# Selective scan with a ternary feed-forward block on one core: softplus, FFN high parts and silus given to other engines

## The reference

```python
xr = x @ in_w.T;  xx, res = split(xr, 2)              # 512 + 512 channels
xx = silu(conv4(xx) + conv_b)                          # causal, 4 taps, per channel
delta, B, C = split(xx @ xproj_w.T, [16, 32])
delta = softplus(delta @ dt_w.T + dt_b)                # 512 channels
state = exp(delta * A) * state + delta * B * xx        # 16 states per channel, 512 steps
y = sum_over_states(state * C) + xx * D
x = layernorm(x + (y * silu(res)) @ out_w.T)
h = silu(lin(x, w1)) * lin(x, w2)                      # ternary weights, 1024 hidden
h = gelu(lin(h, h1)); h = gelu(lin(h, h2))
x = layernorm(x + lin(h, w3))
```

## Time and profile before

| | |
|---|---|
| time, median of 3 runs | 3149.71 us |
| profiled execution: its time, its span | 3155.72 us, 3153.9 us |
| PE busy | 2583.1 us (82%) |
| DVE busy | 2621.1 us (83%) |
| ACT busy | 2343.3 us (74%) |
| POOL busy | 1071.0 us (34%) |
| mean granted clock of TensorE | 0.897 |
| ACT table loads in the profile | 194 |

### The profile page before, as it was taken

How to read it: one execution, slowest core, us unless ns; L and a number is a source line. 1 busy time by engine, 2 the same in 40 slices (tenths; PEclk the granted TensorE clock), 3 DMA queues, 4 the chain that set the end, 5 groups by cost and what they waited for, 6 DMA issues and landing times.

```text
span 3153.9 us, 41504 instructions
## 1 busy us (share of the span) xinstructions
PE 2583.1 (82%) x12290; PEld 1944.8 (62%) x12290; DVE 2621.1 (83%) x2625; ACT 2343.3 (74%) x3653; POOL 1071.0 (34%) x1028
## 2 busy tenths in 40 slices
PE   4355788888888888988888898888888889898888
PEld 1223566676666666676666766666676756666666
DVE  3678998989898897989889898988989898998830
ACT  2776687877969787796968779697877969687822
POOL 0112333333433433343343334234333423423432
PEclk8566899999989999999989999899999989899999
DMA  1996787787878778787887878787787878778933
GB/s 52 290 321 140 167 193 180 185 197 184 194 179 193 190 181 186 183 194 183 190 188 179 194 181 194 179 196 189 178 190 181 200 186 196 189 180 191 229 111 110
DMA packets 230192, 585.49 MB, mean 186 GB/s; under 512 B 26016, under 2 KB 26400, under 8 KB 229808
## 3 DMA queue, kind: packets, MB, share of 16 engines
q0 software_dynamic: 73728, 268.47, 46.2%
q1 hardware_dynamic: 119344, 246.86, 22.4%
q10 hardware_dynamic: 36864, 67.13, 7.9%
HBM read 281.93 MB, written 31.98 MB: 100 GB/s over the span
## 4 chain that ended last, share of the span: by engine, by line
PE 32%; DVE 29%; ACT 17%; issue 14%; DMA 4%; ACTq 1%; DVEq 1%; SPq 1%; POOL 1%; POOLq 0%
PE ffn_ps L479 17%; DVE scan_ps L782 11%; DVE hC L792 5%; PE scan_ps L367 5%; ACT dB L616 4%; ACT dA L607 3%; DVE y L806 3%; PE misc_ps L372 3%; DMA x<-ffn_w 3%; PE misc_ps L423 2%; DVE gate L899 2%; PE misc_ps L460 2%; PE misc_ps L408 2%; ACT L607 2%; PE misc_ps L367 2%
## 5 line engine op out<-in xcount | busy, mean ns | idle before, releaser
L782 DVE TENSOR_TENSOR_SCAN scan_ps<-dA,scan_ps 128x1024 f32<-128x1024 f32 x512 | 1170.8, 2287 | 57.0 <-PE scan_ps L367 33.2
L968 POOL DMA_DIRECT2D y<-hC x512 | 446.1, 871 | 1811.2 <-DVE hC L792 1735.1
L367 PE MATMUL scan_ps<-ident,dB 128*128 128x128 f32 x4096 | 613.4, 300 | 375.7 <-DVE hC L792 292.3
L367 PEld LDWEIGHTS scan_ps<-ident,dB 128*128 128x128 f32 x4096 | 519.9, 154 | 521.2 <-DVE hC L792 305.5
L616 ACT ACTIVATE dB<-duT,bT 128x512 f32<-128x512 f32 x1024 | 726.4, 711 | 154.5 <-PE scan_ps L367 153.2
L607 ACT ACTIVATE dA<-delta,a_neg 128x512 f32<-128x512 f32 (+1 forms) x1024 | 710.1, 712 | 41.1 <-DVE hC L792 38.0
L479 PE MATMUL ffn_ps<-hb_hi,ring 128*128 128x512 f32 x1536 | 660.1, 430 | 18.4 <-DVE gate L899 8.7
L792 DVE TENSOR_TENSOR hC<-scan_ps,c_rows_sb 128x1024 f32<-128x1024 f32 x512 | 623.6, 1218 | 49.8 <-DMA y<-hC 41.5
L479 PE MATMUL ffn_ps<-hb_lo,ring 128*128 128x512 f32 x1536 | 620.7, 404 | 0.0
L479 PE MATMUL ffn_ps<-ha_hi,ring 128*128 128x512 f32 x1024 | 443.5, 433 | 2.4 <-POOL ha_lo L990 2.4
L479 PE MATMUL ffn_ps<-ha_lo,ring 128*128 128x512 f32 x1024 | 407.7, 398 | 0.0
(11 more groups left out here) (90 smaller groups left out, 2941.9 us busy)
## 6 DMA issues: line engine op xcount, KB each, us to landing
y<-hC POOLq DMA_DIRECT2D x512, 512.0 KB, 5.8
ring<-split_weights SPq DMA_DIRECT2D x704, 256.0 KB, 4.3
c_rows_sb<-c_rows ACTq DMA_DIRECT2D x256, 256.0 KB, 4.0
xt<-x_tok SPq DMA_DIRECT2D x32, 512.0 KB, 6.1
x<-ffn_w SPq DMA_DIRECT2D x22, 512.0 KB, 9.7
split_weights<-ha_hi SPq DMA_DIRECT2D x22, 512.0 KB, 5.2
split_weights<-ha_lo SPq DMA_DIRECT2D x22, 512.0 KB, 7.0
out_tok<-out_st SPq DMA_DIRECT2D x16, 512.0 KB, 2.9
```

The costliest lines, as they stand in the source:

```text
L367: mm = nc.tensor.transpose(dst[:, j * P:(j + 1) * P], src(j), ident[:])
L782: nc.vector.tensor_tensor_scan(b, dA[:, a:a + 2, :].rearrange("p a l -> p (a l)"), b, 0.0, ALU.mult, ALU.add).then_inc(scan_done, 1)
L968: pool.dma_start(y2[:, par, c:c + 2, :], hC[:, p % 2], accum_op=ALU.add).then_inc(y_added[p % 2], 16)
```

## The change

Three regroupings, and the tables moved to suit them.

1. Both silus of the mixer use ScalarE's `Silu` and need no DVE product. The convolution's silu is done for four tiles at one step, `F_U` = 38. The halvings of weights that went with tanh are gone.
2. The softplus loses its DVE work except 1+e and its rounding loss. ACT reads dt from PSUM twice, as |x+b| and as relu(x+b). POOL subtracts the loss, adds the ln, multiplies by u, and multiplies u by D.
3. The FFN's high parts are copied by POOL, just before it subtracts them.

```diff
-T_RES, T_GATE = (0, 3, 6, 8), (2, 5, 7, 10)
+T_RES, T_GATE = (2, 4, 7, 9), (4, 5, 9, 10)
-A_HI, A_LO = 2, 3
+A_LO = 2
-LO_AFTER = 1
+LO_AFTER = 0
+F_U = 38
-F_DELTA, F_DELTA_U, F_Y, F_DU = (54, 54, 55, 55), (54, 54, 55, 55), (57, 58, 59, 60), (56, 57, 58, 59)
+F_DELTA, F_DELTA_U, F_Y, F_DU = (52, 52, 53, 53), (53, 53, 54, 54), (57, 58, 59, 60), (56, 57, 58, 59)
-NO_EXP = {s % TILES for s in GELU_AT}
+NO_EXP = {s % TILES for s in GELU_AT} | {F_U} | set(T_GATE)
...
+                if s == F_U:
+                    for c in range(DC):
+                        act.wait_ge(conv_taps, r * (DC * (TAPS - 1)) + (c + 1) * (TAPS - 1))
+                        nc.scalar.activation(y2[:, par, c, :], y2[:, par, c, :], ACT.Silu).then_inc(u_ready, 1)
...
+                if s - 1 in F_DT:
+                    c = F_DT.index(s - 1)
+                    act.wait_ge(pe_dt, r * DC + (c + 1))
+                    nc.scalar.activation(du[:, c, :], misc_ps[:], ACT.Abs, bias=ch[:, c, C_DTB:C_DTB + 1]
+                    nc.scalar.activation(delta2[:, par, c, :], misc_ps[:], ACT.Relu, bias=ch[:, c, C_DTB:C_DTB + 1]
+                                         ).then_inc(dt_ready, 1)
...
-                    nc.scalar.activation(gate[:, c % 2, :], misc_ps[:], ACT.Tanh).then_inc(v_tanh, 1)
+                    nc.scalar.activation(gate[:, c % 2, :], misc_ps[:], ACT.Silu).then_inc(v_ready, 1)
...
+            def front_step(r, par, s):                      # on POOL
+                    if F_SUB[c] == s:
+                        nc.gpsimd.tensor_tensor(delta2[:, par, c, :], delta2[:, par, c, :], du[:, c, :], ALU.subtract
+                    if F_DELTA[c] == s:
+                        nc.gpsimd.tensor_tensor(delta2[:, par, c, :], delta2[:, par, c, :], sp_w[c], ALU.add
+                    if F_DELTA_U[c] == s:
+                        nc.gpsimd.tensor_tensor(du[:, c, :], y2[:, par, c, :], delta2[:, par, c, :], ALU.mult
+                    if F_Y[c] == s:
+                        nc.gpsimd.tensor_tensor(y2[:, par, c, :], y2[:, par, c, :],
+                                                ch[:, c, C_D:C_D + 1].to_broadcast([P, SEQ]), ALU.mult
...
+            def split_tile(f, i):                           # on POOL
+                nc.gpsimd.tensor_copy(hi[:, i % HC, :], x32[:, i % X32, :]).then_inc(ffn_hi, 1)
                 pool.wait_ge(ffn_hi, f * FFN_TILES + (i + 1))
                 nc.gpsimd.tensor_tensor(lo[:, i % HC, :], x32[:, i % X32, :], hi[:, i % HC, :].bitcast(F32),
                                         ALU.subtract).then_inc(ffn_lo, 1)
```

More of the change, by code:

```diff
@@ L629, in front_step @@
                     act.wait_ge(pe_xx, r * DC + (c + 1))
[L630 to L635 removed]
+                    nc.scalar.activation(y2[:, par, c, :], misc_ps[:], ACT.Identity, bias=ch[:, c, C_CONVB:C_CONVB + 1],
+                                         scale=ch[:, c, TAPS - 1:TAPS]).then_inc(conv_base, 1)
+                if s == F_U:
+                    for c in range(DC):
+                        act.wait_ge(conv_taps, r * (DC * (TAPS - 1)) + (c + 1) * (TAPS - 1))
+                        nc.scalar.activation(y2[:, par, c, :], y2[:, par, c, :], ACT.Silu).then_inc(u_ready, 1)
                 if s == F_DBL_OUT:
@@ L643, in front_step @@
                                          ACT.Copy).then_inc(bT_ready, 1)
-                for c in range(DC):
-                    if F_EXP[c] != s:
-                        continue
-                    act.wait_ge(dt_ready, r * DC + (c + 1))
-                    nc.scalar.activation(du[:, c, :], delta2[:, par, c, :], ACT.Abs).then_inc(sp_abs, 1)
+                if s - 1 in F_DT:
+                    c = F_DT.index(s - 1)
+                    act.wait_ge(pe_dt, r * DC + (c + 1))
+                    nc.scalar.activation(du[:, c, :], misc_ps[:], ACT.Abs, bias=ch[:, c, C_DTB:C_DTB + 1]
+                                         ).then_inc(sp_abs, 1)
+                    nc.scalar.activation(delta2[:, par, c, :], misc_ps[:], ACT.Relu, bias=ch[:, c, C_DTB:C_DTB + 1]
+                                         ).then_inc(dt_ready, 1)
                     act.wait_ge(sp_abs, r * DC + (c + 1))
@@ L689, in gelu_tiles @@
                                          scale=fs[:, 2 + i // HC, i % HC:i % HC + 1]).then_inc(gelu_x32, 1)
-            def hi_tiles(f, tiles):
-                for i in tiles:
-                    act.wait_ge(gelu_x32, f * (2 * HC) + (i + 1))
-                    if i == HC:
-                        act.wait_ge(pe_half, f * HALVES + 2 * HC)
-                    dst = hb_hi if i < HC else ha_hi
-                    nc.scalar.activation(dst[:, i % HC, :], x32[:, i % X32, :], ACT.Copy).then_inc(ffn_hi, 1)
             def ffn_step(f, s):
@@ L876, in tail_step @@
             def tail_step(r, par, s):
-                if s in T_GATE:
-                    c = T_GATE.index(s)
-                    dve.wait_ge(v_tanh, r * DC + (c + 1))
-                    nc.vector.scalar_tensor_tensor(out=gate[:, c % 2, :], in0=gate[:, c % 2, :], scalar=1.0,
-                                                   in1=misc_ps[:], op0=ALU.add, op1=ALU.mult).then_inc(v_ready, 1)
                 if s in T_ADD:
@@ L968, in y_pair @@
                 pool.dma_start(y2[:, par, c:c + 2, :], hC[:, p % 2], accum_op=ALU.add).then_inc(y_added[p % 2], 16)
+            def front_step(r, par, s):
+                for c in range(DC):
+                    if F_SUB[c] == s:
+                        pool.wait_ge(dt_ready, r * DC + (c + 1))
+                        pool.wait_ge(sp_lost, r * DC + (c + 1))
+                        nc.gpsimd.tensor_tensor(delta2[:, par, c, :], delta2[:, par, c, :], du[:, c, :], ALU.subtract
+                                                ).then_inc(sp_base, 1)
+                for c in range(DC):
+                    if F_DELTA[c] == s:
+                        pool.wait_ge(sp_base, r * DC + (c + 1))
+                        pool.wait_ge(sp_ln, r * DC + (c + 1))
+                        nc.gpsimd.tensor_tensor(delta2[:, par, c, :], delta2[:, par, c, :], sp_w[c], ALU.add
+                                                ).then_inc(delta_ready, 1)
+                for c in range(DC):
+                    if F_DELTA_U[c] == s:
+                        pool.wait_ge(u_ready, r * DC + (c + 1))
+                        pool.wait_ge(delta_ready, r * DC + (c + 1))
+                        nc.gpsimd.tensor_tensor(du[:, c, :], y2[:, par, c, :], delta2[:, par, c, :], ALU.mult
+                                                ).then_inc(du_ready, 1)
+                for c in range(DC):
+                    if F_Y[c] == s:
+                        pool.wait_ge(pe_dbl, r + 1)
+                        pool.wait_ge(du_ready, r * DC + (c + 1))
+                        nc.gpsimd.tensor_tensor(y2[:, par, c, :], y2[:, par, c, :],
+                                                ch[:, c, C_D:C_D + 1].to_broadcast([P, SEQ]), ALU.mult
+                                                ).then_inc(y_init, 1)
             def gate_tile(r, par, c):
@@ L1013, in iteration @@
                         ffn_step(end, s + TILES)
+                    if front is not None:
+                        front_step(front, fpar, s)
             iteration(-1, 1)
```

82 lines of the change are left out of this document (21 added, 61 removed).

## The result

The changed kernel takes 3212.14 us (median of 4 runs, 3209.38 to 3215.86) against 3150.68 of the kernel before in the same comparison: a ratio of 1.020, with a 95% interval of 1.0182 to 1.0218. It is 61 us slower. The forecast was 26 us slower. The profiled span grew by less, 53.6 us, from 3153.9 to 3207.5: the profiled execution of the kernel before was the slowest of its four.

What follows compares the result with a forecast made beforehand. No engine is full; a cycle of stretches in which engines take turns sets the row. -1.0 + 0.8 + 1.2 = +1.0 us a row, +15 over 15 rows, ends +12: +27, 3176 us on the median's scale, range 3103 to 3232.

Steps and rivals of the forecast that it cites:

- POOL's start: Softplus end: POOL takes the split of tile 6 at about 1351.2, with the gelus ending near 1351.7.
- PE's clock: PE's stretch behind `du`: longer idling makes it begin at half rate, +0.8 us a row, from 0 to 1.9.
- DVE's stretch and the PE stretch: Steps 15 to 31 and 32 to 50: work leaving DVE shortens neither, 0 us a row.
- ACT's earlier gelus: Before the softplus end: copies leave ACT, so the gelus end near 1351.7 instead of 1354.04.
- Softplus end: From the last gelus to `du`: `du` ready 1.0 us a row earlier, from -1.9 to +0.4.
- POOL's chain: Softplus end: two copies, two subtractions, eight operations and one transfer's issue on POOL take 14.8 us.
- Gates: Gate stretch: PE's last projection waits for the third silu, +1.2 us a row, from -1.2 to +3.
- Ends: Start and tail of the program, where nothing hides the chain or the loads: +6.4 and +6 us, together +12.
- Signs: Tests: DVE busy 330 us less, POOL operations 1.25 each, `du` transposes near gelu 7 plus 14.5, 278 loads, PE's silu wait.
- A: Four gate tiles: DVE's part ends the gate stretch, so its relief makes the kernel faster, 3116 us; chance 0.27.
- B: POOL's copy is as dear as its subtraction and the cycle waits for POOL, +3.6 a row, 3216 us; chance 0.15.
- C: ACT's table loads cost a drain beside their row, four in the full stretch adding 5.2 a row, 3255 us; chance 0.03.

Runs made afterwards that it cites:

- Experiment 9: Changed kernel with the subtraction of the rounding loss (four a row) back on DVE: 3197.0 us, 1.0142 of the kernel before.
- experiment 8: Kernel before with the softplus part of the change alone, high parts staying on ACT and gates by tanh: 3195.92 us, 1.0141 of the kernel before.
- Experiment 5: Changed kernel with filler products of constants on PE before its wait for `du`: 3187.65 us with eight, 3178.33 us with four.
- experiments 2 and 4: First: changed kernel with gates back to tanh at the old steps, 3155.98 us. Second: kernel before with only the high parts copied by POOL, 3097.88 us.
- experiment 6: Changed kernel with the gate silus at the steps of the kernel before, and exps allowed at those steps: 3169.78 us, 1.0059 of the kernel before.

## Why the prediction was off

Two steps failed: POOL's start at the softplus end, which was put before gelu 7 ends, and the term for PE's clock, which was too small. By the steps of the prediction, per row and against the table:

- **DVE's stretch and the PE stretch.** DVE's relief was put at nothing in steps 15 to 31, and it is 0.2. ACT's earlier gelus were put at -2.3; measured -2.9. Right, though ACT's list as the prediction counts it is only 1.6 shorter, so the 2.3 stands there without a source.
- **Softplus end.** Forecast: `du` 1.0 earlier than before, so the ln-to-`du` stretch about 1.3 longer. Measured: 3.0 longer. POOL's chain itself was right, 14.8 forecast and 14.8 measured. Its start was wrong. I let it begin 0.5 before gelu 7 ends, and it begins 1.1 behind: POOL had first to get through a split, a subtraction and a transfer's issue, queued behind a wait of 2.3 for DVE's product with C. (Just ahead of that product DVE's rounding loss took 1.66 instead of 0.69 beside a subtraction on POOL, from 1360.17; no run took this away alone.) I had listed what moved to POOL, but not what stood in its list just ahead. Experiment 9 points to the wait, and not to one operation more or less in the queue; the wait itself was not varied. Even with the start as forecast the stretch from the ln to `du` would have been 1.3 longer than before, and experiment 8 shows that POOL's chain costs time also where it starts with the ln. (One bound was miscounted: with the copy at 0.19 the sum gives -1.8, not -1.9.)
- **PE's clock.** This is the term that was mis-sized most. Forecast +0.8, from 0 to 1.9; measured +2.3, above its range. The term was priced from one projection of four matmuls, but the lower level lasted for the whole first part of the stretch, and the wait before it grew to 4.72. Experiment 5 settles it: 34 us of the 61. The trace of before could have told. First the changed kernel behind the softplus end, then the kernel before at the joint that the term was taken from:

```profile
1381.20:1388.00 6.80, 4.84 (x15) 3.96 (x16) 3.63 (x3) 1.81 (x3) 5.70 (x6) 0.50 0.60 120
```

```profile
1294.00:1300.80 6.80, 5.68 (x11) 3.10 (x10) 5.96 (x7) 3.58 (x6) 3.85 (x4) 0.50 0.53 116
```

Both stretches are at half rate throughout (clock 0.50), with PE busy 4.84 us and 5.68 us. Half of that, 2.4 and 2.8 us, is an estimate of what the level costs, where the prediction stopped at the 1.9 of the first four matmuls. The measured cost was 2.4.

- **Gates.** Forecast +1.2, measured +1.7. The mechanism, PE waiting for the third silu, was right: "PE has a wait of 3 to 4 us for the silu before its last projection" is the row with 3.14. That the size is near has some luck in it. By experiments 2 and 4 it is the difference of two larger terms: the silus cost 3.4 and the copies gave back 1.6. From the end of the third silu to the output projection the forecast had 6.9, and in the row shown it is 9.1 (1431.14 to 1440.25), of which 1.6 are the slower projection and transposes; this clock was in the upper bound, not in the sum.
- **Ends.** The start was forecast at +6.4. At the first transposes of `du` the changed kernel is 7.4 behind, but at the first sum behind the output projection only 1.4 (330.8 against 329.4), so most of this is made up within the first row. At the last transposes of `du` it is 51.0 behind, at the end 53.6: the tail, forecast at +6, is +2.6.
- **Signs.** Of those named, 278 loads, eight operations of some 1.25 and the wait for the silu came. The transposes of `du` came 16.0 behind gelu 7, not within 1 us of 14.5, and DVE's busy time fell too little.
- **Rivals.** A (faster) named PE's wait for the silu as its test, and it failed it. B was near in time (3216), but for the wrong reason: the copy is cheap, and layer 1 did not grow. C fell: loads start 0.01 us behind the instruction before, last 1.28, and 32 more of them went with a faster kernel (experiment 6). By "ScalarE: Activation LUTs" of the Trainium skill, "What ACT_TABLE_LOAD costs", a switch would also drain for 1.38 us; no row here shows it.

So +1.0 a row was forecast and +3.95 measured over 11 rows: 1.1 of the miss is the softplus end, 1.5 the clock, 0.5 the gates, less 0.2 for DVE's stretch. Between the first and the last transposes of `du`, 15 rows, it is 2.9 a row, 44 us. What stays open is why single rows of the kernel before differ, between 181.5 and 187.1; no run was made on it.

## What to carry to other kernels

When work is moved to an engine that looks half idle, read its list in order around the new place: what it waits for just ahead of it decides when the work starts, and its mean load says nothing. Price a wait on PE with the matmuls behind it, as long as the clock needs to come back, not only with its own length. And let no instruction that needs a table load stand between another engine and its next work: the four silus cost 3.7 us a row at the late steps and 0.9 at the early ones.
